# A GRU stage whose gate products and normalised input are formed in PSUM

## The reference, cut to what matters

```python
x = x + _L1_gnn_ref(h, ...)          # ends in (h - mu) / jnp.sqrt(var + BN_EPS) * gamma + beta
h = jnp.maximum(_layernorm(x, axis=-1), 0.0)
# _gru_cell(messages, h, ...)
r = jax.nn.sigmoid(i_r + h_r)
z = jax.nn.sigmoid(i_z + h_z)
n = jnp.tanh(i_n + r * h_n)
return (1.0 - z) * n + z * h         # = n + z * (h - n)
```

## Time and profile before

| what | us |
|---|---|
| median of 3 runs | 7526.86 |
| lowest and highest | 7523.41, 7527.03 |
| the profiled execution, whole | 7510.79 |
| its span, first to last instruction | 7509.0 |
| stage P3 in it (first load issued to last out done) | about 1300, from 4846 to 6147 |
| DVE busy in 4900 to 5500 (600 us) | 583.44 |
| POOL, PE, ACT busy there | 550.92, 400.51, 356.24 |

### The profile page before, as it was taken

How to read it: one execution, slowest core, us unless ns; L and a number is a source line. 1 busy time by engine, 2 the same in 40 slices (tenths; PEclk the granted TensorE clock), 3 DMA queues, 4 the chain that set the end, 5 groups by cost and what they waited for, 6 DMA issues and landing times. The chain is left out here.

```text
span 7509.0 us, 103850 instructions
## 1 busy us (share of the span) xinstructions
PE 4833.2 (64%) x21977; PEld 3329.0 (44%) x21977; DVE 4494.6 (60%) x15229; ACT 2867.7 (38%) x6194; POOL 4724.5 (63%) x4658
## 2 busy tenths in 40 slices
PE   3776745568888876236556469866666668854553
PEld 1444433445655656236433247633333334433553
DVE  5866656645745767333322256599999989943210
ACT  0465634434644643231011004465555545543000
POOL 0577766613733757666566307599999978756555
PEclk9998967789999988557788675598999989965766
DMA  2232356678578579446455464333333334433443
GB/s 81 90 107 96 111 168 197 200 234 260 188 237 260 188 219 294 127 132 181 140 111 90 100 198 132 114 126 119 119 117 117 117 120 146 140 91 121 88 70 49
DMA packets 1124708, 1087.87 MB, mean 145 GB/s; under 512 B 106449, under 2 KB 986240, under 8 KB 1124196
## 3 DMA queue, kind: packets, MB, share of 16 engines
q1 hardware_dynamic: 983746, 911.01, 38.5%
q0 software_dynamic: 140800, 175.08, 10.8%
...
## 5 line engine op out<-in xcount | busy, mean ns | idle before, releaser
L2340 PE MATMUL bank<-P_hT,weightsT 128*128 128x512 f32 x1176 | 623.2, 672 | 0.0
L1023 POOL DMA_INDIRECT G_x<-node_table,G_idx x400 | 396.7, 992 | 165.6 <-issue 94.9
L1023 POOL DMA_INDIRECT G_V<-layer_rows,G_idx x400 | 384.6, 961 | 160.8 <-issue 92.2
L1053 PE MATMUL bank<-first_last_indicators,G_V 125*128 (+1 forms) x1600 | 288.2, 302 | 257.2 <-DVE G_V L1702 231.2
L1035 POOL DMA_INDIRECT out<-O_out,O_idx x200 | 315.4, 1577 | 213.2 <-DMA out<-O_out,O_idx 154.6
L1876 PE MATMUL bank<-O_r,O_eq 125*125 125x128 f32 x1600 | 287.9, 364 | 240.4 <-ACT O_out L1902 205.3
L1035 POOL DMA_INDIRECT node_table<-H_out,H_idx x200 | 323.0, 1615 | 169.6 <-DMA node_table<-H_out,H_idx 114.6
L446 POOL TENSOR_TENSOR G_xb<-G_x,b3row 128x512 f32<-128x512 f32 x98 | 125.2, 1279 | 477.8 <-DMA G_x<-x 476.0
L1053 PEld LDWEIGHTS bank<-first_last_indicators,G_V 125*128 125x128 f32 x1600 | 277.3, 261 | 279.2 <-issue 188.0
L1876 PEld LDWEIGHTS bank<-O_r,O_eq 125*125 125x125 f32 x1600 | 280.5, 276 | 247.9 <-issue 162.9
L2202 POOL TENSOR_TENSOR P_d<-P_hT,P_n 128x512 f32<-128x512 f32 x196 | 330.7, 1687 | 92.2 <-ACT P_n L2298 92.2
...
## 6 DMA issues: line engine op xcount, KB each, us to landing
P_x<-node_table SPq DMA_DIRECT2D x196, 512.0 KB
...
BN_g<-node_table SPq DMA_DIRECT2D x195, 256.0 KB
out<-P_out SPq DMA_DIRECT2D x195, 256.0 KB
...
layer_rows<-A_a SPq DMA_DIRECT2D x100, 256.0 KB, 3.7
```

The costliest lines, as they stand in the source:

```text
L1023: pool.indirect_dma_start(out=rows[u][:, c, :], out_offset=None, in_=table, in_offset=bass.IndirectOffsetOnAxis(ap=idx[u][:, c:c + 1], axi ...
L1053: last = nc.tensor.matmul(m.bank[7][:, bass.ds((i * TILE + c) * 2, 2)], V[0:EP, c, :], m.ind[0:EP, bass.ds(i * TILE + c, 1), :].rearrange( ...
L2340: last = nc.tensor.matmul(bank[v % B][:, 0:W], m.w["hh_" + gate], hT[v][:], start=True, stop=not with_m)
```

## The change

P3 gets a function of its own, `gru_dense`; `gru` keeps the B5 stage, with the same instructions in the same order. In `gru_dense`:

- PE makes x1 plus the shift row in PSUM bank bX: one bfloat16 matmul of a ones matrix with `shift_parts` (the shift row split in three bfloat16 parts, made once by `row_parts` on DVE), then x times the identity in float32, four matmuls of 128 columns. POOL's xb is gone; only gA is left there. DVE's x2 adds bX and gA.
- ACT's sigmoid of z is written back to its PSUM bank. DVE multiplies d into the same bank (q) and adds n from there (hnew). The SBUF tiles xb, z and q are gone.
- ACT adds epsilon to the variance (ve, a relu of 128x4) in place of DVE. POOL computes nb in two small steps (mean * rs, then 0 minus that) in place of DVE.
- The order in the bodies is another. DVE: out(i-7), x2(i), stats(i), aggr(i), rn(i-4), q(i-5), hnew(i-5). PE: xb(i+1), T(i-3), back(i-6), gates(i-4). ACT: hT(i-3), n(i-5), h(i-2), r(i-4), z(i-4), ve(i). POOL: gA(i+1), rs(i-1), mr(i-1), nb(i-1), d(i-5). The r gate has one bank where it had two, and bX is one bank.

```diff
+def row_parts(nc, dve, row, rest, piece, parts, s_part):
+    nc.vector.memset(parts[:], 0.0).then_inc(s_part, 1)
+    nc.vector.tensor_copy(piece[0][:], row[:]).then_inc(s_part, 1)
+    dve.wait_ge(s_part, 2)
+    nc.vector.tensor_tensor(rest[0][:], row[:], piece[0][:], ALU.subtract).then_inc(s_part, 1)
+    dve.wait_ge(s_part, 3)
+    nc.vector.tensor_copy(piece[1][:], rest[0][:]).then_inc(s_part, 1)
+    dve.wait_ge(s_part, 4)
+    nc.vector.tensor_tensor(rest[1][:], rest[0][:], piece[1][:], ALU.subtract).then_inc(s_part, 1)
+    dve.wait_ge(s_part, 5)
+    nc.vector.tensor_copy(piece[2][:], rest[1][:]).then_inc(s_part, 1)
+    dve.wait_ge(s_part, 6)
+    for k in range(3):
+        p = slice(32 * k, 32 * k + 1)
+        nc.vector.tensor_copy(parts[p, :].rearrange("p (c f) -> p c f", c=TILE), piece[k][p, :].unsqueeze(1).to_broadcast([1, TILE, D]))\
+          .then_inc(s_part, 1)
 
 
 def load_weights(nc, m, a):
@@ -119,9 +138,11 @@
...
+    m.nil = m.sb("nil", [128, TILE])
...
+    m.ones16 = m.sb("ones16", [128, 128], BF16)
...
+def gru_dense(nc, m, a):
...
+        t, h = (P.slots(k, [128, TILE, D], count=2) for k in ("gA", "h"))
+        hT, nT = (P.slots(k, [128, ROWS], count=4) for k in ("hT", "n"))
+        r, rn, dT, hn = (P.slots(k, [128, ROWS], count=2) for k in ("r", "rn", "d", "hnew"))
...
+        bT, bB, bX, bR = m.bank[0:4]
+        bZ, bN = m.bank[4:6], m.bank[6:8]
...
+            @block.gpsimd
+            def _(pool):
+                def body(i, u, has):
+                    f = Flow(pool, has, m)
+                    if has(i + 1):
+                        v = (u + 1) % 4
+                        f.landed(s_x, i + 1, v)
+                        f.after(s["x2"], i - 1)
+                        nc.gpsimd.tensor_tensor(t[v % 2][:], x[v][:, :, D:2 * D], m.Arow[:].unsqueeze(1).to_broadcast([128, TILE, D]), ALU.mult)\
+                          .then_inc(s["t"], 1)
+                    if has(i - 1):
+                        v = (u - 1) % 4
+                        f.after(s["h"], i - 5)
+                        f.after(s["ve"], i - 1)
+                        nc.gpsimd.tensor_tensor(rs[v][:], ve[v][:], m.minus_half[:], ALU.pow).then_inc(s["rs"], 1)
+                        f.after(s["rs"], i - 1)
+                        nc.gpsimd.tensor_tensor(mr[v][:], mv[v][:, :, 0], rs[v][:], ALU.mult).then_inc(s["mr"], 1)
+                        f.after(s["mr"], i - 1)
+                        nc.gpsimd.tensor_tensor(nb[v][:], m.nil[:], mr[v][:], ALU.subtract).then_inc(s["nb"], 1)
+                    if has(i - 5):
+                        v = (u - 5) % 4
+                        f.after(s["n"], i - 5)
+                        f.after(s["q"], i - 7)
+                        nc.gpsimd.tensor_tensor(dT[v % 2][:], hT[v][:], nT[v][:], ALU.subtract).then_inc(s["d"], 1)
+                sweep(pool, -1, n, n + 4, body, unroll=8, back=7, ahead=1, special=1)
+            @block.vector
+            def _(dve):
+                def body(i, u, has):
+                    f = Flow(dve, has)
+                    if has(i - 7):
+                        v = (u - 7) % 4
+                        f.after(s["back"], i - 7)
+                        f.landed(s_o, i - 11, v)
+                        nc.vector.tensor_tensor(out[v][:], bB[:].rearrange("p (c f) -> p c f", c=TILE), x2[(u - 7) % 8][:], ALU.add)\
+                          .then_inc(s["fin"], 1)
+                    if has(i):
+                        v = u % 4
+                        f.after(s["t"], i)
+                        f.after(s["xb"], i)
+                        f.after(s["h"], i - 8)
+                        nc.vector.tensor_tensor(x2[u][:], bX[:].rearrange("p (c f) -> p c f", c=TILE), t[v % 2][:], ALU.add).then_inc(s["x2"], 1)
+                        f.after(s["x2"], i)
+                        for j in range(TILE):
+                            last = nc.vector.bn_stats(st[v][:, j, :], x2[u][:, j, :])
+                        last.then_inc(s["st"], 1)
+                        f.after(s["nb"], i - 4)
+                        Flow(dve, has, m).after(s["st"], i)
+                        for j in range(TILE):
+                            last = nc.vector.bn_aggr(mv[v][:, j, :], st[v][:, j, :])
+                        last.then_inc(s["mv"], 1)
+                    if has(i - 4):
+                        v = u % 4
+                        f.after(s["r"], i - 4)
+                        f.after(s["n_sum"], i - 4)
+                        f.after(s["n"], i - 6)
+                        nc.vector.scalar_tensor_tensor(rn[v % 2][:], bN[v % 2][:], m.col["bhh_n"], r[v % 2][:], ALU.add, ALU.mult).then_inc(s["rn"], 1)
+                    if has(i - 5):
+                        v = (u - 5) % 4
+                        f.after(s["d"], i - 5)
+                        f.after(s["z"], i - 5)
+                        nc.vector.tensor_tensor(bZ[v % 2][:], bZ[v % 2][:], dT[v % 2][:], ALU.mult).then_inc(s["q"], 1)
+                        f.after(s["q"], i - 5)
+                        f.after(s["back"], i - 7)
+                        nc.vector.tensor_tensor(hn[v % 2][:], bZ[v % 2][:], nT[v][:], ALU.add).then_inc(s["hnew"], 1)
+                row_parts(nc, dve, m.Brow, shift_rest, shift_piece, shift, s_b)
+                sweep(dve, 0, n, n + 6, body, unroll=8, back=11, ahead=0, special=1)
+            @block.scalar
+            def _(act):
+                def body(i, u, has):
+                    f = Flow(act, has)
+                    if has(i - 3):
+                        v = (u - 3) % 4
+                        f.after(s["T"], i - 3)
+                        f.after(s["d"], i - 7)
+                        nc.scalar.activation(hT[v][:], bT[:], ACT.Copy).then_inc(s["hT"], 1)
+                    if has(i - 5):
+                        v = (u - 5) % 4
+                        f.after(s["rn"], i - 5)
+                        f.after(s["hnew"], i - 9)
+                        nc.scalar.activation(nT[v][:], rn[v % 2][:], ACT.Tanh, bias=m.col["bih_n"]).then_inc(s["n"], 1)
+                    if has(i - 2):
+                        v = (u - 2) % 4
+                        f.after(s["nb"], i - 2)
+                        f.after(s["T"], i - 4)
+                        for j in range(TILE):
+                            last = nc.scalar.activation(h[v % 2][:, j, :], x2[(u - 2) % 8][:, j, :], ACT.Relu, scale=rs[v][:, j:j + 1], bias=nb[v][:, j:j + 1])
+                        last.then_inc(s["h"], 1)
+                    if has(i - 4):
+                        v = u % 4
+                        f.after(s["r_sum"], i - 4)
+                        f.after(s["rn"], i - 6)
+                        nc.scalar.activation(r[v % 2][:], bR[:], ACT.Sigmoid, bias=m.col["b_r"]).then_inc(s["r"], 1)
+                        f.after(s["z_sum"], i - 4)
+                        nc.scalar.activation(bZ[v % 2][:], bZ[v % 2][:], ACT.Sigmoid, bias=m.col["b_z"]).then_inc(s["z"], 1)
+                    if has(i):
+                        v = u % 4
+                        f.after(s["mv"], i)
+                        f.after(s["rs"], i - 4)
+                        nc.scalar.activation(ve[v][:], mv[v][:, :, 1], ACT.Relu, bias=m.col["eps"]).then_inc(s["ve"], 1)
+                sweep(act, 0, n, n + 4, body, unroll=8, back=9, ahead=0, special=1)
+            @block.tensor
+            def _(pe):
+                def body(i, u, has):
+                    f = Flow(pe, has)
+                    if has(i + 1):
+                        v = (u + 1) % 4
+                        f.landed(s_x, i + 1, v)
+                        f.after(s["x2"], i)
+                        nc.tensor.matmul(bX[:], m.ones16[:], shift[:], start=True, stop=False, skip_group_check=True)
+                        for c in range(TILE):
+                            last = nc.tensor.matmul(bX[:, c * D:(c + 1) * D], m.ident[:], x[v][:, c, 0:D], start=False, stop=True, skip_group_check=True)
+                        last.then_inc(s["xb"], 1)
+                    if has(i - 3):
+                        v = (u - 3) % 4
+                        f.after(s["h"], i - 3)
+                        f.after(s["hT"], i - 4)
+                        for c in range(TILE):
+                            last = nc.tensor.transpose(bT[:, c * 128:(c + 1) * 128], h[v % 2][:, c, :], m.ident[:])
+                        last.then_inc(s["T"], 1)
+                    if has(i - 6):
+                        v = (u - 6) % 4
+                        f.after(s["hnew"], i - 6)
+                        f.after(s["fin"], i - 7)
+                        for c in range(TILE):
+                            last = nc.tensor.transpose(bB[:, c * D:(c + 1) * D], hn[v % 2][:, c * 128:(c + 1) * 128], m.ident[:])
+                        last.then_inc(s["back"], 1)
+                    if has(i - 4):
+                        v = u % 4
+                        f.after(s["hT"], i - 4)
+                        f.after(s["r"], i - 5)
```

(11 more changed lines are left out.)

155 lines of the change are left out of this document (79 added, 76 removed).

## The result

| | median of the runs | lowest to highest | a group of P3 |
|---|---|---|---|
| before | 7525.1 us | 7518.0 to 7527.0 | 6.50 us |
| changed | 8112.6 us | 8108.5 to 8115.3 | 9.48 us |

The changed kernel takes 1.078 times as long (95% interval 1.0763 to 1.0801). The forecast was 8112 us, with the range 7900 to 8265.

A forecast was written before the change was run, and what follows sets the result against it. VectorE, partly held up by GpSimd, was taken to bound the kernel at 6.50 us a group. An 8.54 us loop plus 0.96 for the low clock gave 9.5; 585 us over 195 groups added to 7526.9 made 8112 us, range 7900 to 8265.

The forecast's parts named there:

- What bounds the kernel before: In P3, VectorE sets the pace at 6.50 us a group, partly held inside instructions by GpSimd's long steps.
- The sums after: Each engine's own work per group in changed P3: none exceeds 4.7 us, so freely running engines would gain.
- The ring: Wait loop x2, xb, T, hT, n, h, r, rn, q, hnew, out, x2 within one group's period: 8.54 us.
- The clock: TensorE's 3.8 us silence lowers its clock; four groups in five hit, 1.2 us each: 9.5 us a group.
- The sum for the stage: P3's added time: (9.5 - 6.50) x 195 = 585 us on 7526.9, giving 8112 us.
- The way beside it: Parallel way from x2 to x2 through TensorE's T, back and gates: 8.18 us, 0.36 to spare.
- The clock stays high: Rival: the same loop in P3 without low clock, 8.54 us a group, 7925 us; chance 0.15.
- The ring does not close: Rival: engines run apart, ports are freed, VectorE's 4.7 us sum sets P3's pace, 7176 us; chance 0.04.
- Every group hit in full, or q dear: Rival: low clock in full every group, or q in PSUM far above 0.68: 10.24 us, 8256 us; chance 0.15.
- What would show it: Signs in P3's profile: x2 starts 1850 us apart, VectorE half busy, idle ahead of rn, TensorE waiting 3.8 us before xb.

The follow-up runs named there:

- the later runs: Kernel with both orders, parts undone: z and q back in SBUF, ratio 0.9517; xb back on GpSimd, 0.9833; all of these, 0.9945.
- the filled run: Changed kernel plus three unneeded float32 matmuls per group on TensorE behind the gates: 7891.9 us, ratio 1.0499.
- both orders: Changed kernel with TensorE reordered to T, gates, back, xb and ScalarE to hT, n, r, z, h, ve: 7166.9 us, ratio 0.952.
- The order experiments: Changed kernel with TensorE's xb moved last: 7445.7 us; with gates also ahead of back: 7168.4 us; with ScalarE's r and z also ahead of h: 7166.9 us.
- the two runs without it: Changed kernel with TensorE's order T, gates, back, xb: 7168.4 us; the same with ScalarE's r and z ahead of h: 7166.9 us.

## Why the prediction was right, point by point

- **What bounds the kernel before.** It was put as VectorE, held up by GpSimd. That is only half of it: the trace of before shows a ring here too, and it goes through the lock. Three of its steps (start us, us):

```profile
5400.82 1.75 DVE L2242 TENSOR_TENSOR P_q<-P_z,P_d 128x512 f32<-128x512 f32 x1
...
5401.99 1.71 POOL L2208 TENSOR_TENSOR P_xb<-P_x,bn_shift 128x512 f32<-128x512 f32 x1
...
5403.28 0.97 DVE L2253 TENSOR_TENSOR P_hnew<-P_n,P_q 128x512 f32<-128x512 f32 x1
```

  Each starts inside the one above it and ends a fixed time after that one's end: q 0.55 us after d, xb 1.13 after q, hnew 0.55 after xb, gA 1.12 after hnew, ve 0.03 after gA. Then VectorE goes on by itself with rn, out and x2, 2.16 us, and d, which has started inside x2, ends 1.12 after it. Together that is the period, 6.66 us, and it is so in all of 156 groups of the middle, within 0.1 us. So the engines meet at this lock too, and not only at semaphores. VectorE's 583 of 600 us were in good part waiting inside instructions. No run takes one step out of this ring: it is read from the trace and not tested. The prediction took VectorE's long q for the loss, which the later runs correct. The forecast did not rest on it.
- **The sums after.** q in PSUM at 0.68: 0.689. ve on ScalarE at 0.30: 0.290. A small GpSimd step at 0.20: 0.203, and 14.1 / 79 = 0.18 us of wait ahead of it. Shift matmul and identity 1.12: in the filled run from 5509.53 to T at 5510.65, 1.12. TensorE's sum 4.7 us: 4.68 us a group with both orders, where TensorE is full. The shift matmul's 0.22 us within it is its place in TensorE's sum; on the ring it was worth about 0.12.
- **The ring.** Each step of it, as put from rows of before, against the period shown: hT to n 0.50 (0.49), n to h 0.63 (0.62), h to r 1.53 (1.54), r with the way to rn 0.71 (0.70), rn to q 0.66 (0.67), q to hnew 0.71 (0.72), hnew to out 0.61 (0.61), out to x2 0.60 (0.60), T to hT 0.63 (0.63 at the high clock). The one term off is x2 done until TensorE starts, 0.15 in the sum and 0.06 in the rows (5509.47 to 5509.53). Sum 8.54, measured 8.48 in the middle of the filled run, where the clock is high, and 8.37 with the filling of the pipeline. The order experiments show that it is this ring.
- **The clock.** 0.96 us a group was chosen, between 0 and 1.70: four groups in five hit, 1.2 us each. In the middle of the stage 128 of 156 were hit, 0.82 of them, at 9.88 - 8.48 = 1.40 us each, together 1.15. Granted clock 0.85 forecast, 0.85 measured. The share was a choice and not a derivation, so that it came out is luck, and why one group in five is spared stays open.
- **The sum for the stage.** Three errors cancel, so that 9.5 against 9.48 looks better than its parts are: the ring 0.06 too long, the clock 0.19 too cheap (1.15 against 0.96), and the filling, which brings the 9.63 of the middle down to 9.48 and which the sum left out when it took 9.5 for all 195 distances.
- **The way beside it.** It was put at 8.18 us at the high clock, 0.36 less than the ring; with r ahead of h, where it is the longest way, x2's short distances are 8.19. But with the low clock it draws level with ScalarE's way (9.86 and 9.88), which the prediction named only as a deduction in the price. It is why putting r ahead of h brought 33 us and not more.
- **The rivals.** The clock stays high (7925): the run with the filler is this rival made real, 7892. The ring does not close (7176): the two runs without it came to 7168 and 7167, bound by TensorE and not by VectorE as the rival had it; the price held because both sums come to about 4.7 us. Every group hit in full, or q dear (8256): q takes 689 ns, and 28 of 156 groups were spared. The first two prices held, so the model of the stage was right in its alternatives too.
- **What would show it.** x2's starts 1849.0 us apart (about 1850, by the cancelling above); VectorE busy for 279 of 600; idle ahead of rn, by ACT's r; q 689, hnew 691, d and gA 1269; TensorE's wait ahead of xb 3.64 us (3.8); clock 0.85. All stand.
